# Graph attention over 8192 nodes on one core: the four quadrant transfers of each adjacency slice in the order 0, 2, 1, 3 instead of 0, 1, 2, 3

## The reference

```
h   = maximum(layernorm(x), 0)                     # 8192 x 256
hid = inlayer2 @ W.T + b                           # 8192 x 128
f1  = hid @ w1 + b1 ;  f2 = hid @ w2 + b2          # 8192 each
logits = f1[:, None] + f2[None, :]
coefs  = softmax(leaky_relu(logits, 0.01) + (-1e9) * (1 - (adj > 0)), axis=-1)
out = x + coefs @ h
```

## Time and profile before

| what | value |
|---|---|
| median of 3 runs | 1506.81 us (1506.67 to 1507.01) |
| the profiled execution | 1505.09 us |
| its span in the trace | 1503.3 us |
| TensorE matmul busy | 1427.8 us, 95% |
| VectorE busy | 1304.9 us, 87% |
| ScalarE busy | 593.6 us, 39% |
| GpSimd busy | 266.6 us, 18% |
| moved by transfers | 302.36 MB, mean 201 GB/s |
| issue to landing of an adjacency transfer, median | 8.9 us |

### The profile page before, as it was taken

How to read it: one execution, slowest core, us unless ns; L and a number is a source line. 1 busy time by engine, 2 the same in 40 slices (tenths; PEclk the granted TensorE clock), 3 DMA queues, 4 the chain that set the end, 5 groups by cost and what they waited for, 6 DMA issues and landing times.

```text
span 1503.3 us, 33329 instructions
## 1 busy us (share of the span) xinstructions
PE 1427.8 (95%) x12585; PEld 1245.0 (83%) x12585; DVE 1304.9 (87%) x1471; ACT 593.6 (39%) x648; POOL 266.6 (18%) x223
## 2 busy tenths in 40 slices
PE   7346999999999999999999999999999999999998
PEld 6234888888888888888888888888888888888887
DVE  6869989898989888898989898989888898989894
ACT  0435343443444344444434343434444444434330
POOL 0347111110111111111111011111111111101111
PEclk9768999999999999999999999999999999999999
DMA  9972999999999999999999999999999999999950
GB/s 299 222 161 60 219 219 220 219 221 216 213 208 208 209 212 210 208 209 207 215 208 209 209 213 209 208 208 213 209 207 209 209 214 206 211 208 212 210 108 11
DMA packets 110164, 302.36 MB, mean 201 GB/s; under 512 B 11716, under 2 KB 44612, under 8 KB 110148
## 3 DMA queue, kind: packets, MB, share of 16 engines
q1 hardware_dynamic: 104016, 296.40, 92.1%
q10 hardware_dynamic: 6132, 5.77, 1.3%
HBM read 293.73 MB, written 8.39 MB: 201 GB/s over the span
## 4 chain that ended last, share of the span: by engine, by line
PE 89%; SPq 4%; DVE 3%; DMA 2%; ACT 1%; issue 0%; POOL 0%; POOLq 0%; ACTq 0%; DVEq 0%
PE acc L734 60%; PE acc L736 30%; SPq L259 3%; DMA adj_sb<-in_adj_dram 1%; DMA H<-in_x_dram 1%; DVE H L556 1%; ACT h_f L389 1%; DVE stats L502 1%; SPq L264 1%; DVE H L555 0%; DVE wgt L570 0%; POOL H L325 0%; DVE h_add L549 0%; DVE wT L459 0%; DVE wT L581 0%
## 5 line engine op out<-in xcount | busy, mean ns | idle before, releaser
L734 PE MATMUL acc<-H,wT 128*128 128x257 f16 x8192 | 1371.0, 275 | 55.6 <-POOL H L325 55.6
L736 PE MATMUL acc<-H,wT 128*128 128x257 f16 x4096 | 1116.4, 273 | 0.0
L734 PEld LDWEIGHTS acc<-H,wT 128*128 128x128 bf16 x8192 | 796.6, 97 | 172.7 <-issue 57.9
L581 DVE STREAM_TRANSPOSE wT<-wgt 128x1024 f32<-128x1024 f32 x512 | 633.9, 1238 | 144.2 <-PE acc L736 144.2
L371 ACT ACTIVATE mask<-adj_sb 128x1024 bf16<-128x1024 int32 x512 | 529.1, 1054 | 569.5 <-DVE wgt L570 449.3
L570 DVE SCALAR_TENSOR_TENSOR wgt<-b_word,c_word,mask 128x1024 f32<-128x1024 f32 x512 | 636.6, 1255 | 0.0
L736 PEld LDWEIGHTS acc<-H,wT 128*128 128x128 f16 x4096 | 405.4, 99 | 53.0
L332 POOL TENSOR_TENSOR x_res<-o_raw,x_res 128x256 f32<-128x256 f32 x64 | 68.1, 1064 | 1133.9 <-ACT o_raw L378 1102.0
L378 ACT ACTIVATE o_raw<-acc,r_den 128x256 f32<-128x256 f32 x64 | 30.4, 474 | 263.7 <-DVE r_den L600 263.7
L337 POOL TENSOR_TENSOR o_sb<-o_sb,x_res 128x256 f32<-128x256 f32 x64 | 83.6, 1307 | 5.3
L334 POOL TENSOR_SCALAR o_sb<-h_mean,no_nb 128x256 f32<-128x256 f32 x64 | 60.1, 939 | 0.0
(11 more groups left out here) (70 smaller groups left out, 95.9 us busy)
## 6 DMA issues: line engine op xcount, KB each, us to landing
adj_sb<-in_adj_dram SPq DMA_DIRECT2D x512, 512.0 KB, 8.9
x_res<-in_x_dram SPq DMA_DIRECT2D x64, 128.0 KB, 4.1
out_dram<-o_sb SPq DMA_DIRECT2D x64, 128.0 KB, 4.5
H<-in_x_dram SPq DMA_DIRECT2D x26, 256.0 KB, 12.8
wgt<-in_L_gnn_inlayer_dram ACTq DMA_DIRECT2D x8, 256.0 KB, 9.6
wgt<-in_L_gnn_inlayer_dram SPq DMA_DIRECT2D x8, 256.0 KB, 10.1
adj_sb<-in_L_gnn_inlayer_dram ACTq DMA_DIRECT2D x8, 256.0 KB, 12.6
adj_sb<-in_L_gnn_inlayer_dram SPq DMA_DIRECT2D x8, 256.0 KB, 13.0
```

Of the source, the lines that this page charges most:

```text
L581: nc.vector.transpose(wT[:, k % 4, :, :].rearrange("p t (g r) -> p g t r", g=Q), wgt[:, c, :, s * SQ:(s + 1) * SQ]).then_inc(t_ready, 1)
L734: pe.matmul(acc[:, par, 0:DV], w_hi[:, k % 4, t, :], H[:, j, part, 0:DV], start=(j == 0 and part == 0), stop=False)
L736: mm = pe.matmul(acc[:, par, 0:DV], w_lo[:, k % 4, t, :], H[:, j, 0, 0:DV], start=False, stop=(j == ROWS - 1))
```

## The change

In `load_adj`, which issues the four quadrant transfers of a slice, the loop over quadrants runs in another order:

```
         def load_adj(eng, I, c):
 
-            for q in range(Q):
+            for q in (0, 2, 1, 3):
                 eng.dma_start(adj_sb[B * q:B * (q + 1), c, :].rearrange("r (g n) -> r g n", g=Q),
                               adj_q[I, c, q]).then_inc(adj_loaded[c], 16)
```

## The result

The changed kernel takes 1503.15 us (median of 20 runs, 1501.68 to 1505.57); the kernel before, on the same chip, 1506.29 us (20 runs, 1504.72 to 1507.27). The ratio is 0.9982 with a 95% interval of 0.9975 to 0.9989: faster by 3.1 us, or 0.18%. The size itself is loose: the 20 runs of before fall into two groups of ten (1504.72 to 1505.90 and 1506.67 to 1507.27 us), and its median lies in the gap between them. By means the gain is 2.7 us (1506.07 and 1503.35).

A forecast was written before the change was run, and what follows sets the result against it. The prediction took TensorE's pace after row tile 1's start as the bound, that start being set by early adjacency loads. Three slices x two crossings x 0.15 us gave 0.9 us off, so a median of 1505.9 us, range 1504.3 to 1507.5 us.

The forecast's parts named there:

- The bound: Whole kernel: the end is the start of row tile 1, plus 63 row tiles at TensorE's 21.27 us, plus a fixed tail.
- What the landing passes on: Row tile 0's end: the ScalarE and VectorE chain shifts as a whole with the landing at 96.76 us, passing on 0.9 us.
- The mechanism: Adjacency transfers: alternating partition halves adds two crossings per slice, each bringing the queue forward; which quadrant lands first is worth nothing.
- 0.15 us per crossing, 0.9 us for six: Early adjacency loads: six added crossings between partition halves save 0.15 us each, moving the last landing from 96.76 to about 95.9 us.
- the three early slices: Both adjacency slices of row tile 0 and the first of row tile 1, queued ahead of 96.76 us: together 0.9 us.
- every slice gives a third: Early adjacency queue: it does not run dry, so the three slices' savings, two crossings each, add up to 0.9 us.
- The range: Whole kernel: 1504.3 to 1507.5 us, holding the forecast's own range and the unmoved case.
- outcome "same": Whole kernel: a change within 0.2%, 3.0 us, which a measurement cannot tell from none; chance 0.86.
- ScalarE's early wait: Sign at row tile 1's first half: ScalarE's wait for this slice falls to 13.7 us from 14.62.
- Row tile 1 started: Sign at TensorE: row tile 1 starts near 156.6 us, where before it was 157.54 us.
- ScalarE's last wait for a first half: Sign in the row tiles after the first: these waits are gone by about 285 us in place of 333.72.

The follow-up runs named there:

- e11: Kernel before with small extra matmuls (fillers) in TensorE's idle stretches, new order in all slices but the three early ones: 1504.78 us, ratio 0.9992.
- e5: Kernel before, old order, with small extra matmuls (fillers) in TensorE's idle stretches of row tile 0 to keep its clock up: 1504.80 us, ratio 0.9991.
- e6: Changed kernel with the same fillers as e5: 1502.69 us, ratio 0.9980.
- e3: Kernel before with quadrant order 0, 1, 3, 2, an exchange inside the upper half: 1505.15 us, ratio 0.9992.
- e4: Kernel before with quadrant order 0, 3, 1, 2, which also alternates halves: 1503.31 us, ratio 0.9982.
- e13: e5 with the new order in the three early slices only: 1503.49 us, ratio 0.9984 to the kernel before.
- e2: Kernel before with the new order in all slices but the three early ones, no fillers: 1505.33 us, ratio 0.9995.
- e1: Kernel before with the new order only in the three early slices, no fillers: 1504.28 us, ratio 0.9986.
- e14: e13 with the new order also in the second slice of row tile 1: 1503.22 us, ratio 0.9981 to the kernel before.
- e15: e13 with the very first slice back in the old order: 1503.74 us, ratio 0.9984 to the kernel before.
- e10: e5 with the new order in the first slice of row tile 1 alone: 1504.69 us, ratio 0.9992 to the kernel before.
- e12: Changed kernel, new order in x strip 3 too, strips 4 to 7 split: SyncE quadrants 0 and 1, ScalarE 2 and 3: 1500.64 us, ratio 0.9967.

## Why the prediction was wrong in its size

- *The bound.* Right. TensorE's steady windows did not change, e11 shows the later slices to be worth nothing, and the end is the start of row tile 1 plus a constant: 1503.3 - 157.54 = 1345.8 us in before and 1503.8 - 158.01 = 1345.8 us in the changed kernel.
- *What the landing passes on.* Right. From the mask to TensorE's last wait it is 54.7 to 54.8 us in before, the changed kernel, e5 and e6.
- *The mechanism.* Right: a crossing from half to half shortens the queue, and whichever quadrant lands first is worth nothing. e3 and e4 show it, and so do the rates from 165 to 205 us, 219 GB/s in before and e3 and 232 and 228 GB/s in the changed kernel and e4.
- *The term that was mis-sized: 0.15 us per crossing, 0.9 us for six.* This failed. With the clock held up the three early slices give 1.3 us (e13) and all slices 2.1 us (e6). The profiled executions say the same: the mask starts at 96.85, 96.59, 96.93, 97.96 and 97.23 us in the five that do not alternate in these slices (before, e2, e3, e5, e11), 97.11 on average, and at 95.66, 94.83, 95.53, 94.55, 93.70 and 95.86 us in the six with an alternating one and unchanged strips (the changed kernel, e1, e4, e6, e13, e14), 95.02 on average. Those 2.1 us are 0.35 us per crossing, or 0.22 us by e13. (The average is rough: the profiled executions of e5 and e11 are among the slowest of their runs, that of e13 among the fastest.)
- *Why it was mis-sized.* I read the price off the one crossing that the old order has in a steady slice, given to 0.1 us, where the queue had just been idle; the early queue had been backed up for tens of microseconds. One slice is too few. The changed kernel seems to show a large gain there too, 6.6 us from the first to the last landing (691.4 + 5.4 to 692.9 + 10.5) in place of 7.4:

```profile
L264 SPq DMA_DIRECT2D adj_sb<-in_adj_dram x4: 317/317/317, 691.4 to 692.9; - x4
DMA to landing us min/median/max: 5.4/8.1/10.5
```

  But over the 94 slices issued from 400 to 1400 us the same two traces have 7.1 us in before and 6.8 in the changed kernel (7.1 in e3, 6.9 in e4): 0.1 to 0.15 us per crossing. The three steps of before are 2.36, 2.51 and 2.23 us on average, so the crossing, the second, is the longest and not the shortest. The 2.4 us that the price was read from was rounding, and that 0.15 us fits such slices was luck.

  Where the queue is backed up a crossing is worth more. From 165 to 213 us the masks of the first halves of two row tiles follow each other by about 20.3 us in before and by 19.1 to 19.5 us with the new order (the changed kernel, e2, e4), 0.2 to 0.3 us for each of four crossings. And between the masks of the first two slices it is 14.5 us in before (14.5 to 14.8 in the six profiled executions with the old order in both) and 14.0 us in the changed kernel (13.8 to 14.1 in the seven with the new order in both and unchanged strips, and 13.9 in e15, which has it in the second alone): 0.3 us for each of two crossings. Why a crossing is worth more in a backed-up queue was not shown.
- *That every slice gives a third.* Borne out roughly by the profiled executions, though not by the pair of before and after alone. The first slice's mask starts at 52.4 us on average in the seven with the old order there and at 51.6 us in the ten with the new one, though both ranges hold the 51.78 us of this pair. From there to the second mask 0.6 us is won, and from the second to the third about 0.9 us (30.4 to 29.5 us on average). The medians agree less well: by e10 the third slice gives nothing by itself.
- *The term that was missing: TensorE's clock at the end of row tile 0.* I had taken the stretch behind the last wait as fixed at 5.88 us. It is 5.88 or about 7.5 us (7.53 in the changed kernel's profile, 7.48 in e1's), by whether the clock stands at its lower level there. The Trainium skill says of this clock (TensorE: Matmul & The Clock Gate, Part 1) that the gate runs freely, so that the same kernel finds it in another phase from run to run. No run here shows the phase. What agrees is that with one and the same chain the stretch has one of two lengths, and that before's runs fall into two groups about 1.9 us apart; the spread of the runs says little, for it is 3.9 us in the changed kernel without fillers, but also 3.5 us in e13 with them. How much of the 3.1 us is the clock's is not shown: the difference of the two orders is 2.1 us with fillers and 3.1 us without by medians, 2.2 and 2.7 us by means, and the scatter allows none.
- *The range.* It allowed for the crossing only what one rounded spacing allowed, 0 to 0.2 us, and nothing for the clock or for a landing that varies by over 1 us from execution to execution. With the 0.22 to 0.35 us that the runs showed, six crossings are 1.3 to 2.1 us. The outcome "same" was borne out narrowly: the change is 0.18%, below the 0.2% named, and clear of noise all the same.
- *The signs in the next profile.* TensorE's windows stayed as they were. ScalarE's early wait was 13.43 us (13.7 forecast). Row tile 1 started at 158.01 us (156.6 forecast), later because of the clock. ScalarE's last wait for a first half fell at 207.56 us, long before the 285 us forecast: here the steady transfers gained more than the 0.6 us per row tile that 0.15 us per crossing makes. One reading under that sign was off by a little as well: from 212.29 to 333.72 us it is six row tiles at the pace of the transfers, 20.24 us, not 5.71 at TensorE's.

## What to carry to other kernels

When one queue fills a tile quadrant by quadrant, alternate between the lower and the upper 64 partitions; it cost nothing here, and it pays only where somebody waits for that queue, here the early loads. Read a price of 0.1 us from the mean of many transfers, and from a stretch in which the queue is as full as where the price will be used: one rounded spacing in a quiet slice gave 0.15 us where 0.22 to 0.35 us was paid. Before sizing an effect of 1 us from one profiled execution, ask how much its landing and TensorE's clock vary from run to run: here each moved the end by more than the 0.9 us forecast, and only many runs showed the gain. Where those runs fall into two groups, look at the mean too, since a median between the groups moves easily. A gain that arrives at an engine in full can still be lost behind it, so compare the stretch behind the last wait as well.

## What the runs showed of the hardware that was not expected

The same three matmuls of 257 columns took 0.33 us and 0.65 us at the two levels of the clock, within one strip of the changed kernel's execution (150.48 to 150.81 us and 151.42 to 152.07 us). The mask that waits for the early slice started between 96.59 and 97.96 us in the profiled executions of before, e2, e5 and e11, which have the same transfers in the same order up to it. A crossing from half to half in one queue was worth 0.1 to 0.15 us where the queue had been idle and 0.2 to 0.35 us where it was backed up, for transfers of 512 KB. And two queues moved 346 GB/s from 30 to 40 us in before, but 226 to 241 GB/s in e12, where they did not keep to one half each.
